# Layer 1's staging of the next image: two of its four steps change engines

## The reference, cut to what matters

```python
x = x + L0(_gn(x))
x = x + L1(_gn(x))          # _gn: group norm, 32 groups of 4 channels
# L1: x_f = fft2(x); gate_B = sigmoid(ifft(gB_f * x_f)); b = ifft(B_f * x_f)
#     b_t = b * gate_B; ... eight steps of a scan in log space ...; h @ W_out + b_out
```

## Time and profile before

| | before |
|---|---|
| median of 3 runs (6856.88 to 6893.54) | 6883.95 us |
| the profiled execution | 6909.09 us |
| its span | 6907.3 us |
| PE busy | 5912.3 us (86%) |
| DVE busy | 4477.4 us (65%) |
| ACT busy | 3641.9 us (53%) |
| POOL busy | 4068.1 us (59%) |
| mean granted TensorE clock | 0.942 |

### The profile page before, as it was taken

How to read it: one execution, slowest core, us unless ns; L and a number is a source line. 1 busy time by engine, 2 the same in 40 slices (tenths; PEclk the granted TensorE clock), 3 DMA queues, 4 the chain that set the end, 5 groups by cost and what they waited for, 6 DMA issues and landing times. The chain is left out here.

```text
span 6907.3 us, 144255 instructions
## 1 busy us (share of the span) xinstructions
PE 5912.3 (86%) x51796; PEld 5278.5 (76%) x51796; DVE 4477.4 (65%) x5283; ACT 3641.9 (53%) x4872; POOL 4068.1 (59%) x3608
## 2 busy tenths in 40 slices
PE   6799999999999999999871378888888888888898
PEld 5678888888888888888761277777777777777787
DVE  6367777777777777777744556666666666666652
ACT  5655556555555555555421355555555555555552
POOL 0146666666666666666671676676666666666640
PEclk8899999999999999999985699999999999999996
DMA  5356667666677666676561589999999899999985
GB/s 129 122 166 208 198 207 216 198 205 201 202 211 209 203 202 201 204 216 205 169 176 50 148 218 247 243 255 249 257 244 255 241 255 255 244 249 250 251 231 154
DMA packets 1239334, 1441.35 MB, mean 209 GB/s; under 512 B 142960, under 2 KB 1025396, under 8 KB 1238516
## 3 DMA queue, kind: packets, MB, share of 16 engines
q1 hardware_dynamic: 1238516, 1431.07, 73.4%
HBM read 999.09 MB, written 431.64 MB: 207 GB/s over the span
## 5 line engine op out<-in xcount | busy, mean ns | idle before, releaser
L1283 PE MATMUL psC<-wide,xhl 128*128 128x256 bf16 x6144 | 1042.9, 280 | 198.6 <-DVE xhl L1451 170.4
L1220 POOL TENSOR_TENSOR stage<-stage,nrow 128x1024 f32<-128x1024 f32 x256 | 652.3, 2549 | 597.7 <-DMA stage<-x_by_block_row 583.0
L1280 PE MATMUL psC<-wide,xhl 128*128 128x192 bf16 x6144 | 868.6, 251 | 0.0
L1237 POOL COPY down<-xhl 48x448 f32<-48x448 f32 x512 | 522.5, 1021 | 545.6 <-PE psC L1289 486.4
L812 POOL TENSOR_TENSOR y<-y,grow 128x1024 f32<-128x1024 f32 x256 | 604.0, 2359 | 323.7 <-DVE y L656 323.7
L1283 PEld LDWEIGHTS psC<-wide,xhl 128*128 128x128 bf16 x6144 | 593.6, 115 | 210.0 <-issue 195.1
L1456 DVE SCALAR_TENSOR_TENSOR xhl<-xhl,psC 128x512 f32<-128x512 f32 x512 | 348.9, 682 | 540.4 <-ACT xhl L1372 539.9
L1387 ACT ACTIVATE hT<-psH 128x512 f32<-128x512 f32 x512 | 305.2, 596 | 700.0 <-PE psH L1325 699.7
L823 POOL TENSOR_TENSOR q<-q,qinv 128x1024 f32<-128x1024 f32 x256 | 490.1, 1914 | 309.4 <-DVE qinv L730 309.4
L1372 ACT ACTIVATE xhl<-psC 128x512 f32<-128x512 f32 x512 | 304.8, 599 | 664.0 <-PE psC L1289 662.5
L1289 PE MATMUL psC<-narrow,down 128*128 128x96 bf16 x6144 | 532.5, 211 | 143.0 <-DMA narrow<-toeplitz_narrow 94.9
(11 more groups left out here) (166 smaller groups left out, 14383.7 us busy)
## 6 DMA issues: line engine op xcount, KB each, us to landing
wide<-toeplitz_wide SPq DMA_DIRECT2D x1024, 140.0 KB, 4.3
xa<-in_x SPq DMA_DIRECT2D x256, 512.0 KB, 4.6
xb<-in_x SPq DMA_DIRECT2D x256, 512.0 KB, 3.8
xc<-in_x SPq DMA_DIRECT2D x256, 512.0 KB, 5.7
x_rows<-xc SPq DMA_DIRECT2D x256, 512.0 KB
res<-x_rows SPq DMA_DIRECT2D x256, 512.0 KB, 7.4
out<-res SPq DMA_DIRECT2D x256, 512.0 KB, 6.4
stage<-x_by_block_row SPq DMA_DIRECT2D x240, 512.0 KB, 7.1
```

The source lines that it names most:

```text
L1220: nc.gpsimd.tensor_tensor(v, v, nrow[:, 0:1, :].to_broadcast([P, NP_, C]), ALU.mult).then_inc(s_scaled, 1)
L1237: nc.gpsimd.tensor_copy(dst[lo, :, :, 0:last], src[lo, :, 0:NQ, CW:])
L1280: nc.tensor.matmul(dst[:, :, :, 2:], lhs, tab[:, :, 32 + part * 12:44 + part * 12], start=False, stop=False)
L1283: nc.tensor.matmul(dst, lhs, tab[:, :, part * 16:part * 16 + 16], start=(n == 0), stop=False)
```

## The change

VectorE now has steps 1 and 2, ScalarE keeps step 3, and GpSimd has step 4. In VectorE's program the scale is at slot 3 st + 6 and the shift at slot 3 st + 7; GpSimd's low part is at slot 3 st + 9. The program of TensorE, ScalarE and SyncE stays as it was, the semaphores they wait for included. `move_down` waits for a count of low parts where it waited for a count of scales, and a new semaphore `s_sub` is raised ahead of each low part in the loop over images.

```diff
         @block.gpsimd
         def _(pool):
-            def scale_stage(n, st):
-                if st == 0:
-                    pool.wait_ge(s_nrow, n * 16 + 16)
-                k = st % STG
-                pool.wait_ge(s_st[k], n * (16 * uses(NST, STG, k)) + 16 * (st // STG + 1))
-                v = stage[k][:]
-                nc.gpsimd.tensor_tensor(v, v, nrow[:, 0:1, :].to_broadcast([P, NP_, C]),
-                                        ALU.mult).then_inc(s_scaled, 1)
+            def low_stage(n, par, st):
+                pool.wait_ge(xh_done, n * NST + st + 1)
+                if not isinstance(n, int):
+                    pool.sem_inc(s_sub, 1)
+                nc.gpsimd.tensor_tensor(half_of(par, 1, st), rows_of(st), half_of(par, 0, st), ALU.subtract
+                                        ).then_inc(xl_done, 1)
...
-                        scaled = (img + 1) * NST + (max(0, min((s - 2) // 3, NST)) if has_stage else 0)
+                        lows = (img + 1) * NST + (max(0, min((s - 7) // 3, NST)) if has_stage else 0)
...
-                    if has_stage and s >= 4 and s % 3 == 1 and s // 3 - 1 < NST:
+                    if has_stage and s >= 9 and s % 3 == 0 and s // 3 - 3 < NST:
                         pool.wait_ge(s_down, img * NBLK + (s + 1) // 2 + DR)
-                        scale_stage(img + 1, s // 3 - 1)
+                        low_stage(img + 1, 1 - par, s // 3 - 3)
...
                     if has_stage and s >= 6 and s % 3 == 0 and s // 3 - 2 < NST:
+                        scale_stage(img + 1, s // 3 - 2)
+                    if has_stage and s >= 7 and s % 3 == 1 and s // 3 - 2 < NST:
                         shift_stage(img + 1, s // 3 - 2)
-                    if has_stage and s >= 10 and s % 3 == 1 and s // 3 - 3 < NST:
-                        low_stage(img + 1, 1 - par, s // 3 - 3)
...
             for st in range(NST):
+                scale_stage(0, st)
                 shift_stage(0, st)
-                low_stage(0, 0, st)
```

More of the change, by code:

```diff
@@ L1037, in layer1 @@
         s_go = sem("d_down_begun")
+        s_sub = sem("d_low_begun")
         s_res = [sem(f"d_res{k}") for k in range(RES)]
@@ L1213, in _, with move_down @@
         def _(pool):
-            def scale_stage(n, st):
-                if st == 0:
-                    pool.wait_ge(s_nrow, n * 16 + 16)
-                k = st % STG
-                pool.wait_ge(s_st[k], n * (16 * uses(NST, STG, k)) + 16 * (st // STG + 1))
-                v = stage[k][:]
-                nc.gpsimd.tensor_tensor(v, v, nrow[:, 0:1, :].to_broadcast([P, NP_, C]),
-                                        ALU.mult).then_inc(s_scaled, 1)
-            def move_down(img, par, blk, scaled):
+            def low_stage(n, par, st):
[4 more added lines that the diff above has]
+                                        ).then_inc(xl_done, 1)
+            def move_down(img, par, blk, lows):
                 pool.wait_ge(s_chain, 3)
-                pool.wait_ge(s_scaled, scaled)
+                pool.wait_ge(xl_done, lows)
                 count = img * NBLK + blk - DR + 1
@@ L1245, in image @@
                     if has_conv and s % 2:
-                        scaled = (img + 1) * NST + (max(0, min((s - 2) // 3, NST)) if has_stage else 0)
+                        lows = (img + 1) * NST + (max(0, min((s - 7) // 3, NST)) if has_stage else 0)
                         if blk + DR < NBLK:
-                            move_down(img, par, blk + DR, scaled)
+                            move_down(img, par, blk + DR, lows)
                         elif has_stage:
-                            move_down(img + 1, 1 - par, blk + DR - NBLK, scaled)
-                    if has_stage and s >= 4 and s % 3 == 1 and s // 3 - 1 < NST:
+                            move_down(img + 1, 1 - par, blk + DR - NBLK, lows)
+                    if has_stage and s >= 9 and s % 3 == 0 and s // 3 - 3 < NST:
                         pool.wait_ge(s_down, img * NBLK + (s + 1) // 2 + DR)
-                        scale_stage(img + 1, s // 3 - 1)
+                        low_stage(img + 1, 1 - par, s // 3 - 3)
             for st in range(NST):
-                scale_stage(0, st)
+                low_stage(0, 0, st)
             for blk in range(DR):
@@ L1435, in _, with scale_stage @@
                     t_.then(nc.vector.tensor_tensor(bias, bias, bias3[:, i, :], ALU.subtract))
+            def scale_stage(n, st):
+                if st == 0:
+                    dve.wait_ge(s_nrow, n * 16 + 16)
+                k = st % STG
+                dve.wait_ge(s_st[k], n * (16 * uses(NST, STG, k)) + 16 * (st // STG + 1))
+                v = stage[k][:]
+                nc.vector.tensor_tensor(v, v, nrow[:, 0:1, :].to_broadcast([P, NP_, C]),
+                                        ALU.mult).then_inc(s_scaled, 1)
             def shift_stage(n, st):
@@ L1441, in shift_stage @@
                                         ALU.add).then_inc(s_normed, 1)
[L1443 to L1446, removed]
             def wrap_stage(n, par):
```

## The result

| | before | after |
|---|---|---|
| median, 8 runs each | 6880.49 us | 6906.1 us |
| ratio, 95% interval | | 1.0048 (1.0031 to 1.0065) |
| the profiled execution (its span) | 6909.09 us (6907.3) | 6891.9 us (6890.1) |
| PE / DVE / POOL busy | 5912 / 4477 / 4068 us | 5875 / 4668 / 3983 us |
| mean granted TensorE clock | 0.942 | 0.949 |

The forecast was 6820 us and faster; the measured time is 25.6 us above the median before. (The profiled execution after is the shorter one, and not by the change: its last stretch, which the change does not reach, took 95 us where the one before took 129 us, nearly all of it at half clock.

A forecast was written before the change was run, and what follows sets the result against it. TensorE sets the pace, kept waiting by VectorE's add, late behind GpSimd's scale. Fourteen images -65, prologue +1, sum -64 us: 6845 us from the profiled 6909.09, or 6820 us against the median 6883.95; range 6760 to 6915 us.

The forecast's parts named there:

- VectorE's wait for the scale: In the fourteen images, VectorE's 309.0 us wait for GpSimd's scale before the shift goes, removing 108 of TensorE's 187 us.
- 60% of 108 arriving: In the fourteen images, 108 us of TensorE's projection waits can go and 60% arrives: -65 us, ends -32 and -108.
- what is late next: In the fourteen images, the filter tables' DMA is late next; TensorE already waits 79.1 us for narrow tables.
- GpSimd's load: GpSimd swaps 16 scales an image for 16 low parts of 2.4 us, ends 1.9 and 3.6: nothing.
- the prologue: Before image 0, only the end grows, by the last low part on slower GpSimd: +1 us, 10 either way.
- image 0: In image 0, GpSimd's work stays the same with a low part at the scale's price: 0, 15 us either way.
- The copies: Copies of `move_down` on GpSimd were read as 0.85 ns a word and 0.18 us fixed, nothing for a run.
- the last rival, the slow low part: GpSimd's low part takes 3.6 us, costing the prologue 20, image 0 20 and the fourteen images 93: 6952 us, chance 0.12.
- the collision moves: GpSimd's low part meets VectorE's scale and shift in the fourteen images; 33 us come back: 6853 us, chance 0.08.
- the 40% that would not arrive: Of 108 us in the fourteen images only 60% was taken, for tables' DMA and low parts meeting other VectorE work.
- prediction's own sign of being wrong: The low part's median over 3.0 us, or TensorE's waits at the projection staying above 150 us.
- The DMA rival: DMA engines hold the pace: projection waits shrink, narrow-table waits grow, some 20% of 108 us is left: 6862 us, chance 0.17.

The follow-up runs named there:

- three-lows run: The changed kernel with three of GpSimd's sixteen low parts of an image, those of slots 12, 36 and 48, one slot later: 6816 us, ratio 0.9898.
- narrow first (all on VectorE, scale first): The changed kernel with low part back on VectorE, scale ahead of the product, and the narrow filter table issued ahead of the wide one: 6809 us, ratio 0.9885.
- three runs with all on VectorE: The changed kernel with low part back on VectorE: alone 6829 us, with scale ahead of the product 6795 us, with narrow tables also issued first 6809 us.
- low-later: The changed kernel with all of GpSimd's low parts one slot later and the wrap at slot 58 instead of 56: 6821 us, ratio 0.9904.
- scale-first: The changed kernel with VectorE's scale put ahead of the product of the same slot: 6817 us, ratio 0.9899.

## Why the prediction was wrong

*What bounds the kernel, VectorE's wait for the scale: right.* The 309 us went, and the shift moved by one slot alone brought 53 us, the three-lows run 1.0% (6875 to 6816 us), against a forecast of 64.

*"-65 us", 60% of 108 arriving: right as a size, for a kernel without the collision, and in part by luck.* The three-lows run took 96 us off the waits at the projection (191 to 95) and 57 off the middle; waits for narrow tables went from 95 to 194 us, as was said of what is late next. But of the 57 us only 40 are idle time of TensorE that is gone (25.9 to 23.0 us an image). The other 17 are shorter busy time, at a half clock of 119 us for 176, which the prediction did not have.

*GpSimd's load and the prologue: right, but one reading on the way was not.* The low part took 2.39 us for 2.4; the prologue was 2.5 us shorter for 1 longer; image 0 -1 for 0. The copies could not show that a run costs nothing, since both have 32 runs; of their fixed 0.18 us up to 5.6 ns could have been each run's, 1.4 us for the low part's 256. The measured 2.39 us shows that it is not so. So the last rival, the slow low part, was not the cause, though it alone had forecast a slower kernel.

*The step that failed is the rival "the collision moves", at 33 us and a chance of 0.08.* It had the mechanism, and its size was made of two guesses: five shifts of sixteen losing 1.4 us, and a third of it reaching TensorE; in the sum itself it was at most a part of the 40% that would not arrive. The runs show three scales, each losing 2.2 us (92 us in fourteen images), and all of it reaching TensorE (93 us less waiting at these slots in the three-lows run), because those scales stand directly ahead of an add. From the changed kernel to the three-lows run the middle is 82 us shorter. The kernel's two programs held the candidates: in slots 12, 24, 36 and 48 VectorE has maximum or clip, scale, add with nothing between, and GpSimd has its low part in the same slot. Slot 24 escapes by 0.35 us, which only the timeline of the changed kernel shows. A mean over the sixteen could not find them. The prediction's own sign of being wrong did come: waits at the projection stayed above 150 us, and scale and shift have means of 1.69 and 1.70 us where 1.3 was named.

*What was not in the sum at all is TensorE's clock.* The row of the late add showed it already: the matmul behind the 2.49 us wait took 0.58 us and not 0.37. Before, the waits at the projection were spread over some nine places of an image; after, 127 of 173 us are gathered into three, with means of 2.2, 3.1 and 3.7 us. The total hardly moved (187 to 173 us) and the half clock went from 176 to 223 us. TensorE's idle gaps grew from 25.9 to 26.2 us an image, 5 us in fourteen, and its busy time by 21 us: the 26 that were lost. So most of the loss is busy time, and an estimate from the clock fits it: at half speed the 47 us more do the work of 23.5. From the changed kernel to the three-lows run the gaps give 45 us and the busy time 38, where the clock's estimate is (223 - 119) / 2 = 52. With narrow first (all on VectorE, scale first) the estimate is 44 us and the busy time rose by 18 only. So that the clock costs is shown by the 12 matmuls for 22; halving its time gave more than the change of busy time in each of these pairs.

*The DMA rival* did not decide the result, but it limits what a repair can bring: 57 of 96 us arrived, and another 143 us came when pieces were loaded to an eighth.

The three runs with all on VectorE have longer middles (2523 to 2529 us) than the low-later and scale-first runs (2516 and 2512 us), though two of the three have lower ratios: their image 0 is shorter (136 to 143 us for 162 and 157). What stays open is what decides, after a given wait, whether the clock falls: 5 of the 28 waits behind slots 12 and 36 had no such stretch near them.

## What to carry to other kernels

Two engines that share an access are timed by their orders and by the moment at which each is ready, not by their loads: ask for each operation that can hold the access which one stands behind it on the other engine, and whether a third engine waits for that one. Then look in the timeline which of the candidates do meet. When a wait is removed by decoupling two operations, the new freedom lets them meet; put the movable one into a slot where nothing waited for stands behind. And count the long waits of TensorE apart from the short ones, since many of the long ones are paid again in clock.

## What the runs showed of the hardware

A GpSimd and a VectorE operation with two SBUF inputs each take turns whole. The one that comes second stands until the first is done (4.03 us where it takes 2.39 alone), and when VectorE has several in a row, GpSimd gets in between two of them: 3.39 us for a scale of 1.2. VectorE's clip, with one SBUF input, takes part too: a low part that begins 0.9 us before its end takes 3.1 us, and the scale behind it 3.4. The add, with one input in PSUM, has a mean of 0.68 us before and after. A GpSimd subtraction with a bf16 input and a bf16 result in runs of four takes 2.39 us, a product all in f32 2.38.

A single wait of TensorE of 2.23 to 2.25 us, with none over 0.15 us in the 8 us ahead of it, was followed within 1.8 us by a stretch at 1.2 GHz in all fourteen images (behind slot 48, changed kernel); in slots 12 and 36 it was 23 of 28 waits of 1.2 to 4.4 us that had such a stretch beginning within a block of them. The stretches last 3.4 us (38 of 52 in the middle) or 6.8 us (14).
